# An LSTM step on one core: the F and O gates computed with the weights stationary, units on partitions, in place of rows that are turned

## What is computed

```python
xW = jnp.einsum('ntd,dk->tnk', x, Wx) + b            # x: 4 x 512 x 256, Wx: 256 x 1024
def step(carry, xw_t):
    prev_h, prev_c = carry
    a = xw_t + prev_h @ Wh                            # Wh: 256 x 1024
    i, f, o = sigmoid(a[:, 0:256]), sigmoid(a[:, 256:512]), sigmoid(a[:, 512:768])
    g = jnp.tanh(a[:, 768:1024])
    next_c = f * prev_c + i * g
    next_h = o * jnp.tanh(next_c)
_, hs = jax.lax.scan(step, (cond, zeros), xW)
return x + transpose(hs, (1, 0, 2))
```

## Time and profile before

| | us |
|---|---|
| median of 3 runs | 1089.95 (1089.76 to 1093.87) |
| the profiled execution | 1090.95 |
| its span, first to last instruction | 1089.2 |

### The profile page before, as it was taken

The page is one execution under the profiler, slowest core; times in us unless marked ns, Lnnn a source line. Parts: engine busy times, 40 slices in busy tenths (PEclk is TensorE's granted clock), DMA queues, the critical chain, the costliest instruction groups (busy, mean ns, idle before and its releaser), DMA issues.

```text
span 1089.2 us, 88137 instructions
## 1 busy us (share of the span) xinstructions
PE 697.3 (64%) x36864; PEld 574.9 (53%) x36864; DVE 790.8 (73%) x4897; ACT 550.4 (51%) x3586; POOL 0.7 (0%) x6
## 2 busy tenths in 40 slices
PE   4666666666666666666666666667666666766664
PEld 3555555555555555555555555555555555545554
DVE  4777777777777777777776777776777777777776
ACT  2455555555545555555554555554545555455554
POOL 0000000000000000000000000000000000000000
PEclk9999999999999999999998999998999998999999
DMA  3000000000000000000000000000000000000000
GB/s 89 5 7 5 6 6 6 6 6 5 7 5 6 7 5 5 6 6 6 6 6 6 5 6 7 5 6 6 6 6 6 6 6 6 5 6 6 6 6 7
DMA packets 32110, 8.74 MB, mean 8 GB/s; under 512 B 31584, under 2 KB 31584, under 8 KB 32096
## 3 DMA queue, kind: packets, MB, share of 16 engines
q1 hardware_dynamic: 31488, 8.41, 3.5%
q10 hardware_dynamic: 608, 0.14, 0.1%
HBM read 6.43 MB, written 2.10 MB: 8 GB/s over the span
## 4 chain that ended last, share of the span: by engine, by line
DVE 51%; PE 24%; ACT 14%; issue 8%; SPq 1%; DVEq 1%; DMA 0%
DVE turned_bank L296 39%; PE gates L364 24%; DVE h_pad L314 8%; ACT tanh_o L212 8%; ACT turned_bank L215 7%; DVE scan_both L301 3%; DVE cell L307 1%; DVEq L330 1%; SPq L139 1%; DVE h_rows L270 0%; DMA wh_raw<-in_L_cond_Wh_dram 0%; SPq L143 0%; DVEq L269 0%; DVE wh L225 0%; DVE wh L222 0%
## 5 line engine op out<-in xcount | busy, mean ns | idle before, releaser
L364 PE MATMUL gates<-wh,h_pad 128*32 128x64 f32 x32768 | 591.2, 227 | 374.8 <-DVE h_pad L314 373.3
L364 PEld LDWEIGHTS gates<-wh,h_pad 128*32 128x32 f32 x32768 | 506.5, 114 | 488.3 <-DVE h_pad L314 486.4
L296 DVE STREAM_TRANSPOSE turned_bank<-gates 128x64 f32<-128x64 f32 x2048 | 478.5, 262 | 182.3 <-PE gates L364 170.0
L203 ACT ACTIVATE tanh_f<-turned_bank 128x8 f32<-128x8 f32 x512 | 90.7, 177 | 438.1 <-DVE turned_bank L296 427.6
L210 ACT ACTIVATE scan_both<-turned_bank 128x8 f32<-128x8 f32 x1024 | 185.1, 181 | 59.9 <-DVE turned_bank L296 17.3
L314 DVE SCALAR_TENSOR_TENSOR h_pad<-tanh_o,turned_bank 128x4 f32<-128x4 f32 x1024 | 132.7, 158 | 74.2 <-ACT turned_bank L215 4.6
L307 DVE TENSOR_TENSOR_SCAN cell<-scan_both 128x12 f32<-128x12 f32 x1024 | 144.0, 181 | 2.1 <-issue 0.3
L215 ACT ACTIVATE turned_bank<-cell 128x4 f32<-128x4 f32 x1024 | 143.3, 172 | 2.5 <-DVE cell L307 0.3
L346 PE MATMUL x_acc<-wx,x_units 128*32 128x128 f32 x2048 | 107.5, 285 | 9.3 <-DVE x_units L249 9.3
L212 ACT ACTIVATE tanh_o<-turned_bank 128x8 f32<-128x8 f32 x512 | 90.7, 177 | 28.9 <-DVE turned_bank L296 6.7
L216 ACT ACTIVATE half_d<-cell 128x8 f32<-128x8 f32 x512 | 100.4, 196 | 0.0
(11 more groups left out here) (24 smaller groups left out, 6.7 us busy)
## 6 DMA issues: line engine op xcount, KB each, us to landing
x_next<-in_x_dram SPq DMA_DIRECT2D x256, 8.0 KB
x_here<-in_x_dram SPq DMA_DIRECT2D x256, 8.0 KB
out_dram<-y_rows SPq DMA_DIRECT2D x256, 8.0 KB
wx_raw<-in_L_cond_Wx_dram SPq DMA_DIRECT2D x8, 128.0 KB, 3.4
wh_raw<-in_L_cond_Wh_dram SPq DMA_DIRECT2D x8, 128.0 KB, 2.7
bias_raw<-in_L_cond_b_dram ACTq DMA_DIRECT2D x4, 32.0 KB, 3.1
h_rows<-in_cond_dram ACTq DMA_DIRECT2D x4, 1.0 KB
```

Of the source, the lines that this page charges most:

```text
L203: nc.scalar.activation(tanh_f[:], of_step(BF, t), ACT.Tanh).then_inc(tanh_f_done, 1)
L296: nc.vector.transpose(turned[k], gates[k][:, 0:W]).then_inc(gates_turned[k], 1)
L364: last = nc.tensor.matmul(gates[k][q * R:(q + 1) * R, 0:W], h_stationary(b, t), wh[:, b, q, columns_of(k)], start=False, stop=b == M - 1, ...
```

## The change

F and O no longer have rows. Each half of F and of O has a PSUM bank of its own, `f_units[m]` and `o_units[m]`, with units on partitions and the 32 (step, sequence) pairs as columns. `units(b, bank, k, m)` loads 32 columns of `wh` as the stationary operand and moves the 4 columns `h_at(b, t - 1)` through it; ScalarE reads the 4 result columns of the step straight from the bank. The x part for these banks is turned once for each chunk (`turn_x_part`) and injected by `inject_units`; that of O follows at t = 0 of the new chunk.

G and I keep their rows (BA, BB) and their turns, which now write to SBUF, as does `tanh_c`. `forget`, tanh_f and tanh_o are split in halves. Orders after the change:

- TensorE: wait for half 0; BA, f_units[0] and G of BB with half 0; wait for half 1; BA, f_units[0] with half 1; I of BB with half 0; BB with half 1; f_units[1]; o_units[0]; o_units[1].
- VectorE: turn of BA, `forget(0)`, turn of BB, `update(0)`, `forget(1)`, `update(1)`, `hidden(0)`, `hidden(1)`.
- ScalarE: tanh_f, then G and I, for half 0 and then half 1; tanh_o, then tanh_c, for half 0 and then half 1; `half_d`.

The x products come in two pieces of 256 columns, behind the products of t = 3 and t = 4; `x_part` is made at t = 6 and its 128 columns of F and O are turned at t = 7.

```diff
-                turn(BF)
                 turn(BA)
+                forget(0)
                 turn(BB)
-                forget()
-                turn(BO)
                 update(0)
+                forget(1)
                 update(1)
                 hidden(0)
                 hidden(1)
```

```diff
+                def units(b, bank, k, m):
+                    at = k * W + m * R
+                    for q in range(Q):
+                        last = nc.tensor.matmul(bank[q * R:(q + 1) * R, t * N:(t + 1) * N], wh[:, b, q, at:at + R],
+                                                h_at(b, t - 1), start=False, stop=b == M - 1,
+                                                tile_position=(0, q * R), skip_group_check=True)
+                    return last
+
                 pe.wait_ge(h_done[0], now)
-                recur(0, BF)
+                rows(0, BA)
+                units(0, f_units[0], BF, 0)
+                rows(0, BB, slice(0, R))
                 pe.wait_ge(h_done[1], now)
-                recur(1, BF).then_inc(gates_done[BF], 1)
-                for k in (BA, BB, BO):
-                    recur(0, k)
-                    recur(1, k).then_inc(gates_done[k], 1)
-                if t == STEPS - 1 and ahead:
-                    pe.wait_ge(x_part_made, chunk + 2)
-                    for k in BANKS:
+                rows(1, BA).then_inc(gates_done[BA], 1)
+                units(1, f_units[0], BF, 0).then_inc(f_done[0], 1)
+                rows(0, BB, slice(R, W))
+                rows(1, BB).then_inc(gates_done[BB], 1)
+                units(0, f_units[1], BF, 1)
+                units(1, f_units[1], BF, 1).then_inc(f_done[1], 1)
+                if t == 0:
+                    for m in range(M):
+                        inject_units(o_units[m], BO, m)
+                for m in range(M):
+                    units(0, o_units[m], BO, m)
+                    units(1, o_units[m], BO, m).then_inc(o_done[m], 1)
+                if ahead and t in X_PRODUCT_AT:
+                    x_product(X_PRODUCT_AT.index(t), chunk + 1)
+                if ahead and t == STEPS - 1:
+                    for k in ROWS:
                         pe.wait_ge(gates_turned[k], now)
-                        inject(k)
-                if ahead and 0 <= t - FIRST_PIECE_AT < len(PIECES):
-                    x_product(*PIECES[t - FIRST_PIECE_AT], chunk + 1)
+                    for m in range(M):
+                        pe.wait_ge(tanh_f_done[m], now)
+                    pe.wait_ge(x_part_turned, chunk + 2)
+                    inject_early()
```

```diff
                 for t in range(STEPS):
                     now = t0 + (t + 1)
-                    act.wait_ge(gates_turned[BF], now)
-                    nc.scalar.activation(tanh_f[:], of_step(BF, t), ACT.Tanh).then_inc(tanh_f_done, 1)
                     for m in range(M):
+                        act.wait_ge(f_done[m], now)
+                        nc.scalar.activation(tanh_f[:, m, :], f_units[m][:, t * N:(t + 1) * N], ACT.Tanh).then_inc(tanh_f_done[m], 1)
                         act.wait_ge(gates_turned[AB[m]], now)
...
-                    act.wait_ge(gates_turned[BO], now)
-                    nc.scalar.activation(tanh_o[:], of_step(BO, t), ACT.Tanh)
                     for m in range(M):
+                        act.wait_ge(o_done[m], now)
+                        nc.scalar.activation(tanh_o[:, m, :], o_units[m][:, t * N:(t + 1) * N], ACT.Tanh).then_inc(o_tanh_done, 1)
                         act.wait_ge(cell_done[m], now)
```

More of the change, by code:

```diff
@@ L26, in lstm_residual_kernel @@
     W = M * R
-    BF, BA, BB, BO = range(4)
-    BANKS = (BF, BA, BB, BO)
-    GC = len(BANKS) * W
+    BA, BB, BF, BO = range(4)
+    ROWS = (BA, BB)
+    GC = 4 * W
     AB = (BA, BB)
@@ L34, in lstm_residual_kernel @@
     WIN = R + N
-    PIECES = [(b, slice(c * GC // 2, (c + 1) * GC // 2)) for b in range(M) for c in range(2)]
-    FIRST_PIECE_AT = 3
+    X_PRODUCT_AT = (3, 4)
+    X_PART_AT = STEPS - 2
+    UNIT_COLUMNS = slice(GC - 4 * R, GC)
     ctx = ExitStack()
@@ L256, in _ @@
             make_x_part(0)
+            turn_x_part(0)
             permute_matrix(wh, wh_raw, 1, 0.5, wh_loaded).then_inc(wh_made, 1)
@@ L290, in step, with forget @@
                     nc.vector.transpose(x_units[:], x_next[:]).then_inc(x_turned, 1)
-                if ahead and t == STEPS - 1:
+                if ahead and t == X_PART_AT:
                     make_x_part(chunk + 1)
+                if ahead and t == X_PART_AT + 1:
+                    turn_x_part(chunk + 1)
                 def turn(k):
                     dve.wait_ge(gates_done[k], now)
-                    nc.vector.transpose(turned[k], gates[k][:, 0:W]).then_inc(gates_turned[k], 1)
-                def forget():
-                    dve.wait_ge(tanh_f_done, now)
-                    nc.vector.scalar_tensor_tensor(out=scan_both[:, :, K * N + K - 1:2 * K * N:K], in0=tanh_f[:], scalar=1.0,
-                                                   in1=half_d[:], op0=ALU.add, op1=ALU.mult).then_inc(forgotten, 1)
+                    nc.vector.transpose(turned[k][:], gates[k][:, 0:W]).then_inc(gates_turned[k], 1)
+                def forget(m):
+                    dve.wait_ge(tanh_f_done[m], now)
+                    nc.vector.scalar_tensor_tensor(out=scan_in[m][:, K * N + K - 1:2 * K * N:K], in0=tanh_f[:, m, :], scalar=1.0,
+                                                   in1=half_d[:, m, :], op0=ALU.add, op1=ALU.mult).then_inc(forgotten[m], 1)
                 def update(m):
                     dve.wait_ge(tanh_ig_done[m], now)
-                    dve.wait_ge(forgotten, now)
+                    dve.wait_ge(forgotten[m], now)
                     nc.vector.tensor_tensor_scan(cell[:, m, :, :].rearrange("p n k -> p (n k)"), scan_in[m][:, 0:K * N],
@@ L339, in _, with x_product @@
         def _(pe):
-            def x_product(b, columns, chunk):
-                opens = (b, columns) == PIECES[0]
-                if opens:
+            def x_product(b, chunk):
+                if b == 0:
                     pe.wait_ge(x_turned, chunk + 1)
                 for q in range(Q):
-                    last = nc.tensor.matmul(x_acc[q * R:(q + 1) * R, columns], x_units[:, b * R:(b + 1) * R],
-                                            wx[:, b, q, columns], start=opens, stop=b == M - 1,
+                    last = nc.tensor.matmul(x_acc[q * R:(q + 1) * R, 0:GC], x_units[:, b * R:(b + 1) * R],
+                                            wx[:, b, q, :], start=b == 0, stop=b == M - 1,
                                             tile_position=(0, q * R), skip_group_check=True)
-                if (b, columns) == PIECES[-1]:
+                if b == M - 1:
                     last.then_inc(x_acc_done, 1)
```

58 lines of the change are left out of this document (39 added, 19 removed).

## The result

| | before | after |
|---|---|---|
| time, median (range), us | 1091.15 (1089.76 to 1093.87) | 2007.05 (2005.76 to 2008.82) |
| ratio to before, 95% interval | 1 | 1.839 (1.835 to 1.843) |
| span of the profiled execution, us | 1089.2 | 2003.6 |
| mean granted clock | 0.963 | 0.572 |
| packets of the queue `q8 instruction` | 9 | 572 |

A forecast was written before the change was run, and what follows sets the result against it. It took the kernel as bound by the chain of one LSTM step, 512 times. From 1090.95: - 74.8 step, + 4.4 loop's end, + 0.6 prologue, - 14 clock = 1007; 1006 from the median, range 975 to 1110.

The forecast's parts named there:

- the longer loop is read again each round: Rival: TensorE's larger loop body doesn't stay, 62 rounds add 2 to 3 us each: 1130 to 1200 us, chance 0.05.
- nothing is read twice: TensorE's code: its queue carries 9 packets over the whole span before the change, so no code is read again.
- a fall in every chunk: Rival: TensorE's clock falls in every chunk for two or three steps: about 1061 us (1030 to 1110), chance 0.15.
- the lower level as the rule: Rival: TensorE runs at 1.2 GHz except in steps with x products: 1180 to 1235 us, chance 0.15.
- about as now: Forecast case: TensorE's clock stays about as before the change (mean 0.963), time 1006 us, chance 0.58.
- clock term of - 14: Whole run: less time lost to TensorE's lower clock level, - 14 us (between - 5 and - 22).
- the prediction's chain: One step, from second h write through F, forget, BB, ig1, scan 1 and tanh_c1 to h write: 1.87 us, gain 0.146.
- the prediction's second estimate: ScalarE's ig1 from SBUF to SBUF: by the Trainium skill's 52 cycles, 0.028 us more than 0.196; sum some 1021.
- the six groups: TensorE's groups between the two h writes: 0.23 us, just fitting because the writes would be 0.23 apart.
- the value chosen near the lower end: TensorE: a group of four passes of 4 or 32 columns costs 0.030 us, between 0.024 and 0.057.
- the rival of 0.057: A 4-column group costs as much as one of 64: step 2.01, 1075 to 1092 us; chance 0.07 with half 0 late.
- half 0 coming late: Rival: scan 0 is held, six groups delay rows(1, BA) by 0.12: some 1068 us; chance 0.07 with group of 0.057.

The follow-up runs named there:

- experiment 3: Kernel after, with a hint at the back edge of TensorE's loop: 1163.52 us, ratio 1.066.
- experiment 5: Kernel after, with the back-edge hint and an unread 256-column filler product at t = 0, 1, 2, 5 and 6: 1089.4 us, ratio 0.997.
- experiment 11: Kernel after, with filler products at t = 0, 1, 2, 5 and 6 and no hint: 2007.63 us, ratio 1.836.
- experiment 6: Kernel before, with an unread filler product at t = 0, 1 and 2: 1066.38 us, ratio 0.974.
- experiments 8 and 9: Kernel after with hint and filler, TensorE's loop head at a block's start (1091.37 us), then ScalarE's and VectorE's too (1092.75 us).

## Why the prediction was wrong

**The loop.** The prediction had the right rival, "the longer loop is read again each round", and the count that it rests on (1,150 to 1,790). What failed is the term that it put at nothing, in two steps. First the chance: "nothing is read twice" was read from 9 packets, and this holds for a body of 1,152 alone; it says nothing of one of 1,790. It belonged among the unknowns, and not at 0.05. Second the price: a round was given one landing of 2 to 3 us. Measured, a round needs 9 packets one behind the other at 3.5 us, which is 31 us, and the products run beside them, not the other way round. The difference to the same kernel with its body kept is 844 us / 62 = 13.6 us a round. The size of the 9 packets (0.15 MB, so 16 KB each) could have warned of it: if 9 of them are all of the 2,304 loads and products in the code, a body half as long again is several packets, not one, and seven landings of 2.7 behind each other would have been 19 us against a chunk of 15.

**The clock.** The prediction said that no row tells which way it goes, put 0.15 each on a fall in every chunk and on the lower level as the rule, and took "about as now". With the code kept (experiment 3) the clock is 0.785, and the steps into t = 0, 3 and 4 have medians of 2.50, 2.30 and 2.52 beside 1.97 to 2.04 for the others: about what "falls in every chunk for two or three steps" describes, neither as now nor the rule. It is worth 74 us (experiment 5), where that rival had 63 (and would have had 69 with its own 2.36 - 1.87 = 0.49 in place of 0.45 for a slow step). The forecast's clock term of - 14 is the second step that failed, with the wrong sign. In the kernel after itself the rise to 0.678 brought nothing (experiment 11).

**The step.** With code and clock out of the way (experiment 5) the new order can be held against the prediction's chain. An ordinary step, t = 2, in the timeline (start, us, engine, line, operation):

```profile
503.45 0.16 DVE L331 SCALAR_TENSOR_TENSOR h_pad<-tanh_o,tanh_c 128x4 f32<-128x4 f32 x1 [0.15 <-ACT tanh_c L225]
504.06 0.25 DVE L313 STREAM_TRANSPOSE turned<-gates 128x64 f32<-128x64 f32 x1 [0.28 <-PE gates L390]
504.15 0.17 ACT L214 ACTIVATE tanh_f<-f_units 128x4 f32<-128x4 f32 x1 [0.63 <-PE f_units L399]
504.34 0.21 ACT L220 ACTIVATE scan_both<-turned 128x8 f32<-128x8 f32 x1
504.36 0.17 DVE L318 SCALAR_TENSOR_TENSOR scan_both<-tanh_f,half_d 128x4 f32<-128x4 f32 x1
504.44 0.24 DVE L313 STREAM_TRANSPOSE turned<-gates 128x64 f32<-128x64 f32 x1
504.47 0.17 ACT L214 ACTIVATE tanh_f<-f_units 128x4 f32<-128x4 f32 x1
504.60 0.70 PE L422 MATMUL spare<-wx,ident 128*128 128x256 f32 x2
504.71 0.21 ACT L220 ACTIVATE scan_both<-turned 128x8 f32<-128x8 f32 x1
504.97 0.18 DVE L324 TENSOR_TENSOR_SCAN cell<-scan_both 128x12 f32<-128x12 f32 x1
505.11 0.16 DVE L331 SCALAR_TENSOR_TENSOR h_pad<-tanh_o,tanh_c 128x4 f32<-128x4 f32 x1
505.19 0.21 ACT L225 ACTIVATE tanh_c<-cell 128x4 f32<-128x4 f32 x1
505.43 0.16 DVE L331 SCALAR_TENSOR_TENSOR h_pad<-tanh_o,tanh_c 128x4 f32<-128x4 f32 x1 [0.15 <-ACT tanh_c L225]
```

| from the second h write, us | predicted | here (median of such steps) |
|---|---|---|
| turn of BA | 0.60 | 0.60 |
| first tanh_f | 0.64 | 0.70 |
| `forget(0)` | 0.85 | 0.90 |
| turn of BB | 0.90 | 0.98 |
| second ig | 1.20 | 1.26 |
| second scan | 1.43 | 1.52 |
| second tanh_c | 1.65 | 1.73 |
| second h write, the step | 1.87 | 1.97 |

The order of events is the predicted one, and each term is a little larger. From the last pass of F to ScalarE it takes 0.12, where the 0.07 of VectorE was assumed (+ 0.05). The turn of BB is 0.08 behind `forget(0)`, not 0.05 (+ 0.03), and takes 0.24 in place of 0.265 (- 0.02). ScalarE's operations from SBUF to SBUF take 0.213 and 0.207, where 0.196 and 0.187 had been taken (+ 0.04); for ig1 that lies between the 0.196 of the sum and the 0.224 of the prediction's second estimate. The terms given for the turn of F in the old step add up to some 0.63 or 0.64, and the row has 0.61, so the working was that far off where a row shows the whole. Against the old order's 2.016 a step (1.974) gains 0.042, and not 0.146. The two h writes are 0.32 apart (505.11 and 505.43), where 0.23 was said: half 0 does come ahead, further than the six groups need.

The view of one line's operations gives the 4-column pass (ns min/median/max):

```profile
L399 PE MATMUL f_units<-h_pad,wh x32: 168/172/190, 503.6 to 504.2; 128*32 128x4 f32 x32
```

0.172 against the prediction's 0.169, and the groups of four passes follow each other every 0.029 to 0.031 up to the middle of `f_units[1]`, where 0.030 was taken. From there through `o_units` they come every 0.040, so the 104 passes take 1.26 where 1.11 was said; the path does not go through the O products. On the path the value chosen near the lower end was right, and the rival of 0.057 is out. So is that of half 0 coming late.

Three kinds of step are longer than the ordinary one, by their medians: the one into t = 0 takes 2.17, since VectorE's loop turn holds the first turn until 0.80 (+ 0.20 where + 0.07 was said), those into t = 5 and 6 take 2.13 and 2.15, and that into t = 2 takes 2.02. By these medians a chunk is 86 us / 64 = 1.34 longer than eight steps of 1.87 and 0.07 for the turn: 512 x 0.104 = 53 for the ordinary step, 64 x (0.16 + 0.18) = 22 for t = 5 and 6, 64 x 0.13 = 8 for t = 0 and 64 x 0.05 = 3 for t = 2. Of these 86, 10 are no loss against the forecast, which carried the old order's own long steps (0.12 at t = 4, 0.04 at t = 6).

There is one more term, and the prediction does not have it: code that is read for the first time. The last chunk stands behind TensorE's loop as code of its own; in experiment 5 it lasts 26.9 us where the others last 16.4, and the DMA view of 1058 to 1085 us has

```profile
q8 instruction: 8, 0.13, 2.1%
```

one in 3.4 us. In experiment 6, whose last chunk has 1,024 loads and products (4 packets), it lasts 16.5. The first chunk, from its first h write on, takes 21.3 against 15.4, and the second 19.7 against 16.4. That is some 20 us, and nearly all that is left of the low clock (slices 2 and 40 of experiment 5) lies in these chunks. So 1006 + 76 + 20 - 8 (what the forecast had left for the clock) is 1094, and 1089.4 was measured (1091.8 in the profiled execution).

The path that was foreseen as gain 75 is 22 on ordinary steps, and the irregular ones take it back: with the clock helped in both, a chunk is 16.37 us in the new order and 16.29 in the old one. The 25 us between the spans of experiments 5 and 6 (1090.0 and 1065.3) are 5 of that and 20 of code read for the first time. That is why even the new order with its code kept and its clock helped only equals the kernel before, and is slower than the old order with the same help.

**What was right:** the x products, the injects, `make_x_part` and SyncE's queue cost the path nothing, as far as the long steps into t = 5 and 6 (open, below) do not come from them; the turn of BA, the 4-column prices on the path and the order of the chain.

In sum: 2007 is 1006 + 83 (the step's terms, and code read for the first time) + 74 (the clock, once the code is there) + 844 (the code read again).

**Open.** In experiments 5, 8 and 9 the second tanh_f of the steps into t = 5 and 6 starts late, here 0.51 behind the first, where an ordinary step has 0.32:

```profile
512.09 0.17 ACT L214 ACTIVATE tanh_f<-f_units 128x4 f32<-128x4 f32 x1 [0.62 <-PE f_units L399]
...
512.60 0.17 ACT L214 ACTIVATE tanh_f<-f_units 128x4 f32<-128x4 f32 x1
```

The passes that it needs ended at 512.29, and ScalarE's ig before it at 512.49. TensorE's O products beside it last 0.67 in place of 0.48, with 0.145 between two passes of one group (512.370 and 512.515), so more than ScalarE is held. Placing is ruled out (experiments 8 and 9). Experiment 3, without fillers, has 2.04 and 1.97 at these two steps, so the fillers may have a part in it; none was taken away singly.

## What to carry to other kernels

Count the instructions in one round of each engine's loop, not the work in them: here the passes of a step went from 64 to 104 and the loop from 1,152 to 1,792, while the columns streamed in a step fell from 4,096 to 2,304. Where the queue of instructions shows more packets than the code has blocks, the loop is read again, and its rate (here 256 instructions in 3.5 us) is a bound like any engine's. In the kernels here a hint at the back edge helped a body of 1,792 and hardly one of 2,304: hint the back edge, look at the packets again, and only then judge the change itself. Where the granted clock is below 1 and TensorE has room ahead of its next wait, a product that nobody needs may pay, as it did in the kernel before (1066 in place of 1091).

## What the chip showed unexpectedly

- Code is read one packet of 16 KB after another, 3.5 us each on average, though these packets take only 2.1% of the time of the 16 DMA engines.
- Whether a body is read again is not a matter of its size alone: 1,792 gave 572 packets, the same with its head at a block's start 113, with the hint 14. With 2,304 the hint changed 348 to 319. At 1,664 and 1,792 (head moved) a round read all 9 packets or none.
- Code that runs once is read at the same rate: the last chunk of the new order, 7 or 8 packets, took 26.9 us in place of 16.4.
- In the kernel after, a higher clock brought nothing: up from 0.572 to 0.678 and the same 2007 us.
- From a pass's end to ScalarE's start it is 0.12 us, to VectorE's 0.07.
- The best kernel run here is the one before, with three filler products a chunk and the loops of ScalarE and VectorE placed: 1063.0, 2.8% below it.
